# Layer-norm statistics of the next rows: two row tiles in a batch's last step and two in its first, deviations in the first step, rows fetched one batch ahead

## The reference

```python
x = L0_attn_x                                  # (8, 512, 512) float32
xn = _layernorm(x, axis=-1)                    # (x - mean) / sqrt(var + 1e-5)
s = _L0_attn_ref(xn, Wqkv, b_qkv, Wout, b_out) # 16 heads of 32, ALiBi bias, causal softmax
g = _silu(_L0_ffn_ref(xn, w_router, w_fc, w_proj))  # 2 experts, top-1 by softmax(x @ w_router.T)
x = x + s * g
```

## Time and profile before

| what | value |
|---|---|
| time of three runs | 1479.03, 1481.97, 1482.86 us; median 1481.97 |
| the profiled execution's own time | 1481.51 us |
| its span, first to last instruction | 1479.7 us |
| mean granted TensorE clock | 0.987 of full speed |
| `xin<-in_x` DMAs, issue to landing | 4.4 us (median of 32) |

### The profile page before, as it was taken

One profiled execution on the slowest core, in us unless ns is written; L12 is line 12 of the kernel. 1 busy time (PEld: TensorE's weight loads), 2 busy tenths in 40 slices (PEclk: granted clock), 3 DMA queues, 4 the chain that ended last, 5 costly groups with the idle time before them and its releaser, 6 DMA issues.

```text
span 1479.7 us, 30039 instructions
## 1 busy us (share of the span) xinstructions
PE 1384.0 (94%) x9863; PEld 880.8 (60%) x9863; DVE 923.9 (62%) x2441; ACT 770.7 (52%) x1824; POOL 682.5 (46%) x896
## 2 busy tenths in 40 slices
PE   2889999999999999999689999999999999999995
PEld 1455555655555565555456666666666666666663
DVE  7577777777777777777759745555444555544444
ACT  3478778787777878787736422222222222222221
POOL 0356667465666746566523433333333333323332
PEclk9989999999999999999999999999999999999998
DMA  4425334343534434245346311110011111010100
GB/s 161 144 86 148 125 115 125 110 139 100 171 101 130 128 106 138 89 141 140 107 164 207 115 44 44 44 43 25 23 41 42 39 44 44 30 29 30 36 30 30
DMA packets 84897, 133.45 MB, mean 90 GB/s; under 512 B 14095, under 2 KB 63247, under 8 KB 82576
## 3 DMA queue, kind: packets, MB, share of 16 engines
q1 hardware_dynamic: 75808, 105.70, 23.0%
q0 software_dynamic: 8944, 25.83, 5.6%
HBM read 97.81 MB, written 33.95 MB: 89 GB/s over the span
## 4 chain that ended last, share of the span: by engine, by line
PE 75%; DVE 10%; POOL 6%; ACT 3%; issue 3%; DMA 1%; DVEq 1%; SPq 0%; ACTq 0%; POOLq 0%
PE psY L1126 19%; PE psF L1106 19%; PE psA L352 19%; PE psT L446 7%; PE psA L461 5%; POOL pr L941 4%; PE psS L425 3%; DVE sg L1303 2%; PE psX L1080 1%; POOL route L969 1%; PE psA L409 1%; DVE stat L749 1%; DVE am L636 1%; ACT stage L519 1%; DVE wf L1225 1%
## 5 line engine op out<-in xcount | busy, mean ns | idle before, releaser
L1106 PE MATMUL psF<-xT,wf 128*128 128x256 f16 (+1 forms) x3264 | 368.0, 269 | 0.0
L1126 PE MATMUL psY<-wf,aT 128*128 x1584 | 363.9, 379 | 0.3 <-DVE aT L1270 0.3
L1106 PEld LDWEIGHTS psF<-xT,wf 128*128 x3264 | 312.0, 98 | 63.5
L1344 POOL TENSOR_TENSOR a<-a 128x512 f32<-128x512 f32 (+1 forms) x136 | 153.1, 1126 | 392.1 <-DVE a L1261 390.5
L941 POOL TENSOR_SCALAR pr<-pr,rden 128x128 f32<-128x128 f32 (+3 forms) x512 | 268.4, 542 | 141.9 <-DVE rden L868 140.3
L579 ACT ACTIVATE pr<-pr,mn 128x128 f32<-128x128 f32 (+3 forms) x512 | 281.9, 553 | 0.0
L857 DVE CUSTOM_DVE_ANT_0 pr<-psS,base,nsl 128x128 f32<-128x128 f32 (+3 forms) x512 | 249.6, 543 | 4.2 <-PE psS L425 4.2
L1126 PEld LDWEIGHTS psY<-wf,aT 128*128 128x128 f16 x1584 | 154.5, 98 | 158.5 <-issue 1.0
L446 PE MATMUL psT<-conf,pr 128*128 128x128 f32 x1280 | 205.7, 279 | 18.1 <-POOL pr L941 16.5
L1183 ACT ACTIVATE rl<-psF 128x512 f32<-128x512 f32 (+1 forms) x136 | 79.3, 583 | 263.2 <-PE psF L1106 263.0
L446 PEld LDWEIGHTS psT<-conf,pr 128*128 128x128 f32 x1280 | 157.3, 143 | 81.3 <-POOL pr L941 27.3
(11 more groups left out here) (155 smaller groups left out, 1371.0 us busy)
## 6 DMA issues: line engine op xcount, KB each, us to landing
qk_parts<-pre SPq DMA_DIRECT2D x64, 256.0 KB, 2.8
qs<-qk_parts SPq DMA_DIRECT2D x128, 128.0 KB, 2.7
ks<-qk_parts SPq DMA_DIRECT2D x128, 128.0 KB, 2.7
wst<-in_wf SPq DMA_DIRECT2D x16, 1024.0 KB
wstage<-in_wf SPq DMA_DIRECT2D x32, 512.0 KB, 4.6
xin<-in_x SPq DMA_DIRECT2D x32, 256.0 KB, 4.4
attn_out<-so SPq DMA_DIRECT2D x32, 256.0 KB, 2.0
pt<-in_wqkv SPq DMA_DIRECT2D x4, 768.0 KB, 10.1
```

The costliest lines, as they stand in the source:

```text
L1106: last = nc.tensor.matmul(psF[c % 2][:, k * TT:k * TT + tn], w(e, 2 * hc, hl, kc * 512 + col, P), xT[:, r % 2, x, kc, 0:tn], start=(m == 0 ...
L1126: last = nc.tensor.matmul(psY[r % 2][h][:], aT[:, c % 4, x, k, h * P:(h + 1) * P], w(e, 2 * hc + 1, hl, q * 512, 512), start=(c == 0 and k ...
L1344: nc.gpsimd.tensor_tensor(at, at, at, ALU.mult).then_inc(s["a_ready"], 1)
```

## The change

The change moves the statistics of tiles 0 and 1 of a batch one step ahead, to step 15 of the iteration before, and those of tiles 2 and 3 from step 1 to step 0. POOL's `veps` and `rstd` go from step 1 to step 0. Since the rows are now read in step 15, SP fetches them earlier: iteration b fetches batch b + 2, behind the stack of the fourth group and ahead of the stores of the output of batch b - 1. Each fetch waits until `xn` of batch b + 1 has been made from the same buffer. In iteration -1 DVE does all four tiles of batch 0 in step 0, as it did in steps 0 and 1, with nothing between. The number of instructions is the same on each engine.

```diff
@@ att_sync @@
         def iteration(b, odd):
-            if within(b, 0, B - 1):
-                for i in range(QB):
-                    wait(sp, s["xn_ready"], b * QB + i + 1, s["apart_sp"])
-                    sp.dma_start(xin[:, i, :], io["x"][bass.ds((b + 1) * S + i * P, P), :]
-                                 ).then_inc(x_in[i], 16)
...
             if within(b, 0, B):
                 stack(b, 3)
+            if within(b, -1, B - 2):
+                for i in range(QB):
+                    wait(sp, s["xn_ready"], (b + 1) * QB + i + 1)
+                    sp.dma_start(xin[:, i, :], io["x"][(b + 2) * S + i * P:(b + 2) * S + (i + 1) * P, :]
+                                 ).then_inc(x_in[i], 16)
@@ att_vector @@
-            def ln_stats(i):
-                wait(dve, x_in[i], (nxt + 1) * 16)
+            def ln_stats(batch, i):
+                wait(dve, x_in[i], (batch + 1) * 16)
                 link(nc.vector.bn_stats(stat[:, i, :], xin[:, i, :]))
                 nc.vector.bn_aggr(mv[:, i, :], stat[:, i, :]).then_inc(s["ln_stats"], 1)
...
                 turned(2)
-                if more:
-                    if step < 2:
-                        ln_stats(2 * step)
-                        ln_stats(2 * step + 1)
-                    elif step < 6:
-                        ln_apply(step - 2)
+                if b == -1 and step == 0:
+                    ln_stats(0, 0)
+                    ln_stats(0, 1)
+                if more and step == 0:
+                    ln_stats(nxt, 2)
+                    ln_stats(nxt, 3)
+                if more and 2 <= step < 6:
+                    ln_apply(step - 2)
+                if within(b, -1, B - 2) and step == 15:
+                    ln_stats(b + 2, 0)
+                    ln_stats(b + 2, 1)
@@ att_gpsimd @@
-                if more and step == 1:
+                if more and step == 0:
                     wait(pool, s["ln_stats"], (nxt + 1) * QB, s["apart_pool"])
```

More of the change, by code:

```diff
@@ L732, in weight_scales @@
             ts(x(X_CY), x(X_CY), 2.0 ** -8, None, ALU.mult).then_inc(s["scaled"], 1)
-        LINKS = 17
+        n_link = [0]
         def iteration(b, odd):
@@ L738, in iteration @@
             more = within(b, -1, B - 1)
-            k = [0]
             def link(ins):
-                k[0] += 1
+                n_link[0] += 1
                 ins.then_inc(s["dve_link"], 1)
-                wait(dve, s["dve_link"], (b + 1) * LINKS + k[0], s["apart_dve"])
-            def ln_stats(i):
-                wait(dve, x_in[i], (nxt + 1) * 16)
+                dve.wait_ge(s["dve_link"], n_link[0])
+            def ln_stats(batch, i):
+                wait(dve, x_in[i], (batch + 1) * 16)
                 link(nc.vector.bn_stats(stat[:, i, :], xin[:, i, :]))
@@ L918, in iteration @@
                     ffn["split_lo"](dve, range(4 + step // 2, 5 + step // 2))
-            assert not more or k[0] == LINKS, k[0]
         batches(dve, iteration)
```

## The result

| | before | after |
|---|---|---|
| median time | 1482.86 us (7 runs, 1479.03 to 1484.03) | 1488.46 us (7 runs, 1486.07 to 1489.36) |
| ratio, 95% interval | 1 | 1.0040 (1.0029 to 1.0051) |
| span of the profiled execution | 1479.7 us | 1484.3 us |
| a turn of the loop, iterations 1 to 6 | 85.47 us, six times | 86.10 us three times, 87.77 us three times |

The account below looks back on a forecast made before the run. TensorE, busy 94%, was taken as the bound, with gains only where it waits for POOL and DVE. Six boundaries of +0.47 us less 0.6 for iteration 0 gave +2.2: 1484.2 us on the median, range 1478 to 1488.5.

Parts of the forecast that it names:

- X4: Start of PE's step 4 in a steady turn; forecast 0.47 us later at each boundary.
- Two statistics ahead of the cast: Step 15: two statistics sets on DVE push the `cx` cast, for which POOL's `cx` waits, back by 1.60 us.
- X1: Start of PE's step 1; forecast late behind head 1's `pr`, a new stall of about 1.0 us.
- Deviations in step 0: POOL's `veps` and `rstd` ahead of head 2's `pr`; step 0's statistics expected in time, costed at nothing.
- X2: Start of PE's step 2; forecast 1.45 us later than before, with a second, small stall.
- X3: Start of PE's step 3; forecast 1.2 us earlier than before, with no wait for `pr` or `mn`.
- Chain from C to X4: Step 2, from DVE's CAST of the q product (C) through `xn`, cast, `cx` and head 4's `pr`: 5.66 us.
- the slower rival: DVE's CAST stretches head 1's or 2's `pr` to 2.70 us; +1.12 each boundary, 1488.1 us; chance 0.20.
- Iteration 0: First iteration, without `cx` in these steps; X4 at 85.9 instead of 86.48, so -0.6 us, once.
- `xn` did meet `pre`: Rival that step 2's `xn` does not meet POOL's `pre`: -0.25 each boundary, 1479.9 us; chance 0.15.
- step 15 did not swallow the statistics: Rival that step 15 absorbs them and X1 does not move: -0.7 each boundary, 1477.1 us; chance 0.12.
- the length that the rule asks for: Rival that step 2's `xn` is held for all of `pre`: 0.25 more each boundary, 1485.7 us; chance 0.05.

Follow-up runs that it names:

- e2: Changed kernel with step 15's two statistics behind the `cx` cast instead of ahead of it; 1476.09 us, ratio 0.9972.
- e9: Changed kernel plus six useless products at the start of step 4, where PE waits anyway; 1482.31 us, ratio 1.0017.
- e12: Changed kernel plus three useless products at the start of step 1, in the 0.78 us wait; 1486.15 us, ratio 1.0037.
- e13: Second run of the changed kernel with six useless products at the start of step 4, unedited; 1484.01 us, ratio 1.0020.
- e1: Kernel before with only the fetch of the rows moved, statistics and deviations where they were; 1481.22 us, ratio 1.0000.
- e6: Changed kernel with step 2's `xn` behind the `cx` cast instead of ahead of it; 1480.33 us, ratio 1.0000.
- e5: Changed kernel with step 15's statistics behind the `cx` cast and deviations in step 1 between `pr` and `pre`; 1476.73 us, ratio 0.9976.
- e3: Changed kernel with the deviations back at the end of step 1; 1480.52 us, ratio 1.0001.
- e10: Kernel before with only the fourth context's `cx` moved from step 2 to step 1; 1477.38 us, ratio 0.9977.
- e8: Changed kernel with step 15's statistics behind the cast, deviations between step 1's `pr` and `pre`, fourth `cx` in step 1; 1463.94 us, ratio 0.9896.

## Why the prediction was off

Its chain from step 15 to X4 held step by step; one of its terms was too small, and one, the clock, was missing. The missing one weighs more.

- *Two statistics ahead of the cast*: +1.60 at the cast; the view gives -0.36 and +1.25 behind X0, +1.61. POOL's `cx` moved by 1.43 (forecast 1.44 to 1.60), X1 by 0.85, with a wait of 0.78 (forecast about 1.0). Right, at the lower end: cast and `pr` were at their short durations, 0.40 and 2.05. e2 shows it from the other side.
- *Deviations in step 0*: X2 +1.26, forecast +1.45, wait 0.24. The statistics of step 0 were there in time: DVE's fourth set ends about 499.9, POOL comes to `veps` at 501.68. Cost nothing, as said.
- *X3*: -1.35, forecast -1.2, no wait there. Right. The short wait for `mn`, which I expected to go, stands a step later (514.04).
- *Chain from C to X4*: C, the CAST, is 509.74, exactly X2 + 4.53. POOL's `cx` starts 2.37 behind it, by the sum 2.39. `xn` took 1.28, foreseen as 1.27. **The term that was mis-sized is head 4's `pr`: 2.05 in the sum, 2.48 measured**, so the chain is 6.05 instead of 5.66 and X4 is +0.67 instead of +0.47. I took it from rows with no CAST and no `xn` of DVE beside; here those of step 3 lie beside it, and I had the row of a `pr` with such company at 2.70 in the earlier trace rows. I used it for head 1 and 2 alone, in the slower rival. X2, which came 0.19 earlier than taken, gives half of the 0.39 back. The term makes 6 x 0.20 = 1.2 us of the miss.
- *Iteration 0*: -0.6 forecast; -0.5, from the four profiles with the changed order and no fall or other disturbance there (e2, e9, e12, e13: 80.81 to 80.87) against e1 with the old one (81.36). The sum is near, the way is not quite the one forecast: X2 is 1.55 later, not 1.3, and X4 only 0.26 earlier, not 0.6; the other 0.25 us is won in step 4 (6.55 against 6.81), which I had not looked at. So the total is in part luck.
- *Fetch*: 0, e1.
- **The term that was missing is TensorE's clock.** The forecast moved a stall of 1.80 us from X3 to one at X4 (about 1.6 forecast, 1.36 measured) and priced it at its length; that the granted clock could fall behind it was put at nothing, without a reason. With the profile's three falls of 1.68 it costs 5.0 us more. Without falls the sum is 6 x 0.64 - 0.5 = +3.3 us, 0.22%, which would not have been told from no change; the kernels with the wait filled give 1.0017 and 1.0020, +1.9 and +3.5 us. What is over this in the changed kernel, 1.0038 and 1.0040, goes with the falls.

Of the rivals, the slower one named the right side and nearly the size (1488.1), for a cause that did not come: head 1's `pr` took 2.05 and head 2's 2.06. `xn` did meet `pre`, and step 15 did not swallow the statistics. `xn` was not held for the length that the rule asks for: it ended 0.29 behind `pre`, in e6 the cast did too, which alone takes 0.40. The Trainium skill (SBUF — State Buffer, section Who interferes with whom) says that the engine that issues second is fully blocked. Both rows agree that the second one ends only behind the first; neither has it run its whole length from there.

**Open.** Why a fall follows in some turns and not in others. At X4 of the changed kernel no fall came without the wait ahead of it (e9, e13, with e12 as control), but the wait is not enough: e2 has it six times and no fall, e5 six times and two falls, e3 has more waiting and none, and before has 1.80 us six times and none in these iterations, while e1 with the same turn has one (iteration 1, step 3, 5.96 instead of 4.28) and e10 another (iteration 4, step 3, 5.81). Nor is the place special: before, e6 and e10 have a fall in step 4 of iteration 0, where PE waits for `mn`. Every fall looked at stands behind a wait of 1.06 to 1.81 us; what else it takes, no run here shows. Nor was it measured how many falls a timed execution has. That before's own executions have about one each would explain that e2, e3, e6 and e8 came out 0.5 to 2.5 us better than their turns say; this is argued, not shown.

## What to carry to other kernels

Work of 1.6 us that is moved to where its engine seems idle costs its place in the queue: put it behind the instruction that another engine waits for, not ahead (0.97 us a turn here, from loss to gain). When one late place is mended, follow the queues to the next one and take out of that chain what needn't be in it; two edits worth 0.70 and 0.20 us alone were worth 1.87 together. Price an instruction from a row with the same company on the other engine, and give it a range (a head's `pr` beside a CAST and an `xn` took 2.22 to 2.70 us), and a stall of TensorE at more than its length, until the granted clock behind it has been seen.

## What the runs showed of the hardware

- After a wait of TensorE of 1.36 us, which ends a stretch with shorter ones (0.78, 0.24 and 0.34), the granted clock was at the 1.2 GHz level for some 3 us in three turns of six (in each of three profiles), for 1.68 us each. Six useless products in the wait removed it (twelve turns of twelve in two profiles); three products in a wait of 0.78 us, 15 us earlier, did not. A wait of 1.37 us in e2 was followed by no fall in six turns.
- A DVE instruction of 0.40 (cast) or 0.53 us (`xn`) that is issued 0.17 us into a POOL subtraction of 1.16 us ends 0.29 us behind it, whichever of the two it is: 1.28 us.
- Four POOL multiplications of 2.05 us together take 2.48 beside a CAST of 0.43 and an `xn` of 0.54 on DVE, and 2.22 where that CAST took 0.80 (e6). Which of the two takes longer differs from case to case.
